# A two-layer graph network beside a mixing branch: all mixing moved into layer 0's gathers, the second layer finished tile by tile between the quads of its own gathers

## The reference

```
xn = layernorm(x)
# gnn, twice (W0, then W1), on xn:
  agg[r] = sum over edges (r, c) of v[c];  deg[r] = max(number of edges of r, 1)
  v = silu(layernorm((v + agg / deg) @ W.T + b) * g + beta)
# mix, on xn, row by row: logmap of xn, a 256 x 768 product with batchnorm folded in, relu,
  a grouped 128 x 128 product, an attention over groups of 32 channels,
  a 512 x 256 product, a tanh of the row's norm
x2 = x + gnn(xn) + mix(xn)
# ffn, on layernorm(x2): logits (6250 x 8 x 64), softmax, 8 x 64 slice tokens summed over ALL rows,
  a small attention between the tokens, and the result spread back over the rows
out = x2 + ffn
```

## Time and profile before

| | |
|---|---|
| median of 3 runs | 2936.33 us (2932.64 to 2941.06) |
| the profiled execution | 2949.13 us, of which the span from the first to the last instruction is 2947.2 us |
| first gather of layer 0 | 298.3 us |
| last product of layer 0 ends | 1308.0 us |
| first gather of layer 1 | 1432.0 us |
| last product of layer 1 ends | 2439.8 us |
| slice sums complete | 2799.6 us |
| mean granted TensorE clock | 0.873 of full speed |

### The profile page before, as it was taken

How to read it: one execution, slowest core, us unless ns; L and a number is a source line. 1 busy time by engine, 2 the same in 40 slices (tenths; PEclk the granted TensorE clock), 3 DMA queues, 4 the chain that set the end, 5 groups by cost and what they waited for, 6 DMA issues and landing times.

```text
span 2947.2 us, 34117 instructions
## 1 busy us (share of the span) xinstructions
PE 2224.6 (75%) x8923; PEld 1618.1 (55%) x8923; DVE 1404.6 (48%) x3188; ACT 1624.0 (55%) x3910; POOL 1645.6 (56%) x1745
## 2 busy tenths in 40 slices
PE   0776677777778787669487778778787658899999
PEld 0542456565656665555355656566565545455577
DVE  8899513443434443327523434344343215899611
ACT  7410465666666666536556666666666533565422
POOL 0000777777777777740477777777777771344300
PEclk9887688998888898878788989888898876899999
DMA  7200333333333333351333333333333347200002
GB/s 181 70 18 0 98 109 109 114 109 112 113 113 110 114 111 108 111 145 46 114 109 109 113 112 111 111 113 114 111 110 110 109 113 174 72 18 9 1 18 70
DMA packets 101271, 280.80 MB, mean 95 GB/s; under 512 B 29211, under 2 KB 43369, under 8 KB 97088
## 3 DMA queue, kind: packets, MB, share of 16 engines
q0 software_dynamic: 75904, 210.74, 25.1%
q1 hardware_dynamic: 12184, 55.08, 7.0%
q10 hardware_dynamic: 13000, 12.80, 1.5%
HBM read 252.91 MB, written 25.60 MB: 95 GB/s over the span
## 4 chain that ended last, share of the span: by engine, by line
POOL 50%; PE 17%; issue 17%; DVE 14%; DMA 1%; ACT 1%; DVEq 0%; ACTq 0%; SPq 0%; POOLq 0%
POOL big L566 50%; PE ps L1161 3%; PE ps L1262 3%; DVE arena_a L1296 3%; DVE arena_a L1297 3%; PE ps L1128 2%; PE ps L1150 2%; PE ps L1042 1%; PE ps L1144 1%; PE ps L1254 1%; PE ps L1159 1%; DVE big L1733 1%; DMA big<-table,arena_a 1%; DVE big L1734 1%; DVE lnst L1340 1%
## 5 line engine op out<-in xcount | busy, mean ns | idle before, releaser
L566 POOL DMA_INDIRECT big<-table,arena_a x1568 | 1509.6, 963 | 709.1 <-issue 476.7
L1042 PE MATMUL ps<-big 128*125 x3968 | 1073.5, 431 | 504.0 <-SPq L461 308.0
L1042 PEld LDWEIGHTS ps<-big 128*125 128x125 f32 x3968 | 833.3, 214 | 716.7 <-issue 565.4
L1629 DVE TENSOR_TENSOR big<-ps,big 125x257 f32 x496 | 211.0, 425 | 1263.5 <-PE ps L1042 1240.4
L697 ACT ACTIVATE arena_b<-iota_row,arena_a 128x125 f32<-128x125 f32 x1984 | 601.3, 386 | 62.2 <-PE ps L1042 28.2
L699 ACT ACTIVATE big<-arena_b,ones 128x1000 f32<-128x1000 f32 x248 | 280.0, 1129 | 8.1
L720 ACT ACTIVATE nodes<-nodes 125x512 f32<-125x512 f32 x50 | 31.6, 632 | 305.1 <-DVE nodes L1687 305.1
L1683 DVE RECIPROCAL nodes<-nodes 125x512 f32<-125x512 f32 x50 | 167.7, 3353 | 1.7
L1061 PE MATMUL ps<-arena_b,nodes 128*125 128x384 f32 x400 | 165.4, 538 | 0.0
L594 POOL TENSOR_TENSOR arena_b<-arena_b,head 125x512 f32<-125x512 f32 x50 | 55.0, 1100 | 161.9 <-DVE head L1741 161.9
L555 POOL IOTA big<- 1x992 f32 x1 | 0.9, 948 | 195.0 <-DVEq L1419 195.0
(11 more groups left out here) (387 smaller groups left out, 3159.7 us busy)
## 6 DMA issues: line engine op xcount, KB each, us to landing
big<-table,arena_a POOLq DMA_INDIRECT x1568
table<-nodes SPq DMA_DIRECT2D x9, 1120.0 KB
nodes<-table SPq DMA_DIRECT2D x4, 1680.0 KB
nodes<-table ACTq DMA_DIRECT2D x50, 125.0 KB
mix_rows<-nodes ACTq DMA_DIRECT2D x50, 125.0 KB
nodes<-in_x_dram SPq DMA_DIRECT2D x5, 1120.0 KB
big<-mix_rows SPq DMA_DIRECT2D x5, 1120.0 KB
nodes<-in_x_dram SPq DMA_DIRECT2D x10, 560.0 KB
```

What stands on the lines that cost most here:

```text
L566: pool.indirect_dma_start(gat[:, GRP * slot + k, 0:D], None, table[l], bass.IndirectOffsetOnAxis(ap=s_dst[:, n:n + 1], axis=0)).then_inc(s ...
L1042: mm = pe.matmul(ps[0:PT, SUM_BANKS[q % SB], 0:257], onehot[:, ROUND * (r % 2) + QS * k + n, :], gat[:, bass.ds(slots[QS * k + n], 1), :]. ...
L1629: dve.tensor_tensor(at, ps[0:PT, SUM_BANKS[q % SB], 0:257].unsqueeze(1), at, ALU.add).then_inc(s("agg_added"), 1)
```

## The change

Five things change together.

1. **Tiles are ranked by edge count.** After the layer norm's statistics VectorE makes the sizes of the tiles from the counts (ScalarE counts 33 bounds, VectorE 16 more), compares all 50 x 50 pairs, and for each tile makes a 125 x 800 bfloat16 mask times its rank, which TensorE adds up by 100 products with a unit matrix (`take_ranks`). The keys of the sort are built from these ranks, so levels 1 to 7 of the sort move behind all this and behind the row factors that followed the statistics. Small tiles come first. Idle quads are placed so that in layer 1 the tile of rank k is complete after 5 (k + 1) quads (`QUADS_A_TILE`).
2. **All 50 mixing tiles go into layer 0** (`NM = NT`). `window` now runs over 124 half rounds: two quads, then one slot, 111 slots in all. ScalarE makes its one-hot matrices two groups ahead. `mix_slot` keeps its steps, its order and its waits on all engines.
3. **Between the layers** the row factors of mixing and the weights of the logits are prepared, before TensorE's first quad of layer 1.
4. **Layer 1 goes tile by tile.** A list of 272 turns is worked out when the program is built (`second_layer_plan`). Each turn has one quad (as long as there are any, 248), and then steps of some tiles, in a fixed order: W slice sums, N division, M maximum, subtraction and exponential, L logits, D transpose for them, C scaled x2, Q and V second layer norm's roots, X x2, Z scale and tanh, R and S first layer norm's roots, B its statistics, H product with W1, T transpose, U agg / deg + x. Layer 1's quads have two banks (6, 7) in place of four; T, H and D share bank 5, L has bank 4 alone. GpSimd's division goes to VectorE. Each tile's rows of the layer-1 table, of x and of mixing are loaded by ScalarE's queue, and x2 is stored to DRAM by it. Part of the list (letter and rank):

The core of the diff:

```diff
-SUM_BANKS = (3, 4, 5, 7)
-SB = len(SUM_BANKS)
-IDLE_LOG = 12
-IDLE_STEP = 82
-assert 0 <= 50 * IDLE_STEP * NQ - NQ * 2 ** IDLE_LOG < 2 ** IDLE_LOG
+SUM_BANKS = ((3, 4, 5, 7), (6, 7))
+QUADS_A_TILE = 5
+SUMMED = 34
+EQ_RING = 4
 NSG = NSL // GRP
...
-NM = NT // 2
-EARLY = (0, 3)
+NM = NT
+HALVES = 2 * NSL // ROUND
+AHEAD = 2
...
+STAGES = ("W", "N", "M", "L", "D", "C", "Q", "V", "X", "Z", "R", "S", "B", "H", "T", "U")
+PE_COST = {"W": 1.9, "L": 1.0, "D": 0.35, "H": 1.4, "T": 0.35}
+DVE_COST = {"N": 1.6, "M": 1.5, "X": 1.8, "Z": 1.1, "S": 1.5, "V": 1.5, "B": 0.45, "U": 0.6}
+X1_RING, BASE_RING, XL_RING = 3, 3, 3
+
...
+                if st == "U" and tick < min(QUADS_A_TILE * (k + 1), NQ) - 1:
+                    break
+                if items and (pe + PE_COST.get(st, 0) > 2.3 or dve + DVE_COST.get(st, 0) > 3.1):
+                    break
+                if any(s0 == st for s0, _ in items) and st not in "SRVQ":
+                    break
+                pe, dve = pe + PE_COST.get(st, 0), dve + DVE_COST.get(st, 0)
+                at[st, k] = tick
+                items.append((st, k))
+                nxt[st] += 1
...
+def window(step, slot):
+
+
+    for half in range(max(HALVES, SLOTS)):
+        if half < HALVES:
+            step(half)
+        if half < SLOTS:
+            slot(half)
...
+                rows_dma(sp, x2_all[:, 10 * k:10 * k + 10, :], x2_d[:, 10 * k:10 * k + 10, :], s(f"nodes_back{k}"))
...
+            tile_of = tile_numbers(mybir.EngineType.SP)
+            for k in range(NT):
+                tile = tile_of(k)
+                sp.wait_ge(s("out_ready"), k + 1)
+                for p in PARTS:
+                    sp.dma_start(out_d[p, tile, :], x2_all[p, k, :].unsqueeze(1)).then_inc(s("out_stored"), 16)
...
+                def onehots_ahead(half):
+                    if half == 0:
+                        for grp in range(AHEAD):
+                            onehots(grp)
+                    if half + AHEAD < NSG:
+                        onehots(half + AHEAD)
...
+                def second_step(st, k):
+                    if st == "T":
+                        act.wait_ge(s("u_turned"), NT + k + 1)
+                        if k >= 2:
+                            act.wait_ge(s("h_made"), NT + k - 1)
+                        act.activation(uT_two[:, 2 * (k % 2):2 * (k % 2) + 2, :],
+                                       ps[:, 5, 0:D].rearrange("p (k c) -> p k c", k=2)[:, :, 0:PT], ACT.Copy).then_inc(s("bank5_read"), 1)
...
+                    if st == "C":
+                        act.wait_ge(s("xl_scaled"), GROUP_OF[k] + 1)
+                        if k >= XL_RING:
+                            act.wait_ge(s("w_used"), k - XL_RING + 1)
+                        act.activation(xl_ring[:, k % XL_RING, 0:D], acc[:, k, 0:D], ACT.Identity,
+                                       bias=xl_shift[:, k:k + 1], scale=cols[:, 2, k:k + 1]).then_inc(s("xl_ready"), 1)
...
+                    if st == "M":
+                        act.wait_ge(s("shifted"), k + 1)
+                        act.activation(ffw[:, k, :, :], ffw[:, k, :, :], ACT.Exp).then_inc(s("exp_done"), 1)
...
+                    if at >= len(banks):
+
+                        pe.wait_ge(s("agg_added"), q - len(banks) + 1)
...
+                    if st == "H":
+                        pe.wait_ge(s("bank5_read"), max(BANK_READS[st, k] - 1, BANK_READS["T", k]))
+                        pe.matmul(ps[0:PT, 5, 0:D], ones3[:, 0:PT], gbias3[1][:, :], start=True, stop=False)
+                        for n in range(2):
+                            mm = pe.matmul(ps[0:PT, 5, 0:D], uT_two[:, 2 * (k % 2) + n, :], wT[1][:, n, :], start=False, stop=(n == 1))
+                        mm.then_inc(s("h_made"), 1)
...
+                    if st == "L":
+                        pe.wait_ge(s("bank5_read"), BANK_READS["D", k])
+                        if k >= 1:
+                            pe.wait_ge(s("shifted"), k)
+                        pe.matmul(ps[0:PT, 4, :], ones3[:, 0:PT], lbias3[:, :], start=True, stop=False)
+                        for n in range(2):
+                            mm = pe.matmul(ps[0:PT, 4, :], xlT_ring[:, n, :], wc[:, n, :], start=False, stop=(n == 1))
+                        mm.then_inc(s("logits_made"), 1)
...
+            for t in range(SUMMED, NT):
+                link(dve.tensor_scalar(eq_ring[2 + t % 2], bin_b, float(t), 0.0, ALU.is_lt, ALU.add, accum_out=counts[0:PT, t:t + 1]))
...
+                link(dve.tensor_tensor(less, order.unsqueeze(1).to_broadcast([P, NT, NT]), order.unsqueeze(2).to_broadcast([P, NT, NT]), ALU.is_lt))
+                link(dve.tensor_reduce(rank, less, AX.X, ALU.add))
+                dve.sem_inc(s("ranks_ready"), 1)
+                for t in range(NT):
+                    if t >= EQ_RING:
+                        dve.wait_ge(s("eq_used"), t - EQ_RING + 1)
+                    dve.tensor_scalar(eq_ring[t % EQ_RING], bin_b, float(t), rank[0:PT, t:t + 1], ALU.is_equal, ALU.mult).then_inc(s("eq_made"), 1)
...
-                        dve.wait_ge(s("agg_made"), q + 1)
-                        dve.tensor_tensor(at, ps[0:PT, SUM_BANKS[q % SB], 0:257].unsqueeze(1), at, ALU.add).then_inc(s("agg_added"), 1)
...
+                    if st == "X":
+                        base = x_ring[:, k % BASE_RING, :]
+                        dve.wait_ge(s(f"base_row{k % BASE_RING}"), 32 * (k // BASE_RING + 1))
+                        do.mark(dve.scalar_tensor_tensor(out=base, in0=mix_ring[:, k % BASE_RING, :], scalar=by_rank[:, 0, k:k + 1], in1=base,
+                                                         op0=ALU.mult, op1=ALU.add))
+                        dve.wait_ge(s("tanh_done"), k + 1)
+                        do.mark(dve.scalar_tensor_tensor(out=row, in0=th_ring[:, k % 2, :], scalar=1.0, in1=row, op0=ALU.add, op1=ALU.mult))
+                        do.wait()
+                        dve.tensor_tensor(row, row, base, ALU.add).then_inc(s("x2_made"), 1)
+                        dve.wait_ge(s("x2_made"), k + 1)
...
+                    if st == "M":
+                        dve.wait_ge(s("logits_made"), k + 1)
+                        link(dve.tensor_reduce(head8[:, k % 2, 0, :], heads(ps[0:PT, 4, :]), AX.X, ALU.max))
+                        dve.wait_ge(s(f"x2_stored{k % 2}"), 16 * (k // 2 + 1))
+                        dve.tensor_tensor(each, logits, per_head(0).unsqueeze(3).to_broadcast([PT, 2, H // 2, G]), ALU.subtract).then_inc(s("shifted"), 1)
+                    if st == "N":
+                        dve.wait_ge(s("exp_done"), k + 1)
+                        link(dve.tensor_reduce(per_head(1), each, AX.X, ALU.add))
+                        link(dve.reciprocal(head8[:, k % 2, 2, :], head8[:, k % 2, 1, :]))
...
+                    for tick, items in enumerate(PLAN):
+                        if tick < NQ:
+                            addition(tick)
+                        for st, k in items:
+                            second_step(st, k, tick)
```

More of the change, by code:

```diff
@@ L170, in group_due, with roots_due, h_bank @@
     return g if rest == 0 and 0 <= g < NT // 10 else None
[L173 to L183, removed]
+def roots_due(i):
+    return 1 + min(max((i - (LN_Z - 2)) // 10 + 1, 0), NT // 10)
+def h_bank(a):
+    return 3 if a % 2 == 0 else 7
 def live(i, lag, n=NT):
@@ L414, in run_halves, with tile_numbers, tile_of @@
             return g[:, :, 0:gap], g[:, :, gap:2 * gap]
+        def tile_numbers(engine):
+            held = {}
+            def tile_of(k):
+                part = k // 16
+                if part not in held:
+                    held.clear()
+                    _, held[part] = nc.values_load_multi_w_load_instructions(
+                        order_row[0:1, part * 16:min(part * 16 + 16, NT)], [engine], min_val=0, max_val=NT - 1,
+                        skip_runtime_bounds_check_because="a tile's number, a sum of one-hot products")
+                return bass.ds(held[part][k % 16], 1)
+            return tile_of
         block = ctx.enter_context(nc.Block())
@@ new lines, in _ @@
+            sp.wait_ge(s("ffn_loaded"), 8 * 16)
+            tell_landed(1, 0)
+            for first in range(0, NGRP - RG, 16):
+                quads_before = free_slots(1, first)
+                for grp in range(first, min(first + 16, NGRP - RG)):
+                    tell_landed(1, grp + 1)
+                    sp.wait_ge(s("agg_made"), quads_before[grp - first])
+                    sp.sem_inc(s("slots_free"), 1)
+            for grp in range(NGRP - RG + 1, NGRP):
+                tell_landed(1, grp)
@@ L819, in post_slot @@
+                        act.activation(nodes[:, b, :], acc[:, b, 0:D], ACT.Silu).then_inc(s("silu_done"), 1)
                     a = tile_at(i, 1)
                     if a is not None:
[L821 to L827 removed]
@@ new lines, in _ @@
+                if l == 0:
+                    window(products, mix_slot)
+                    pe.wait_ge(s("gw_ready"), 4)
```

(11 more changed lines are left out.)

956 lines of the change are left out of this document (533 added, 423 removed).

## The result

The changed kernel takes 3030.78 us (median of 4 runs, 3012.33 to 3031.4) where the kernel before takes 2938.69 beside it: a ratio of 1.030, interval 1.026 to 1.034. I forecast 2885 with a range up to 2985 and gave a slower kernel 0.26. The sign is wrong and the time lies outside the range.

What follows compares the result with a forecast made beforehand. GpSimd's gathers were taken to bound both gather stages. The terms 50 + 155 + 30 - 283 - 3 gave -51 us, so 2885 us against the median of 2936.3, with a range of 2795 to 2985.

Steps and rivals of the forecast that it cites:

- Preparation, +50: Before the first gather: counts, tile ranking and masks make the stage 50 us longer, bounds +38 and +65.
- Layer 0's gathers, +155: Layer 0's gather stage, now with all 50 mixing tiles, grows by 155 us, bounds +105 and +270.
- a tenth more on 9.1: 19.7 us: Layer 0's period per mixing tile: TensorE's 9.1 us cost a tenth more for its clock, making 19.7 us.
- the circle: Layer 0's loop of waits through ScalarE, TensorE and VectorE: 18.7 us per tile at full clock, above the supply of 16.0.
- Layer 1's gathers, +30: Layer 1's gather stage, with mixing gone and the old end moved in, grows by 30 us, bounds 0 and +120.
- turns slower than gathers: Rival, chance 0.24: layer 1's turns take 4.5 us in the mean, not 4.0, costing 120 instead of 30: 2975 us.
- 30 turns take 113 against 120: Layer 1, from turn 111: thirty turns need 113 us against 120 of gather supply, so gathers still set the pace.
- turns 111 to 121: Layer 1's turns, some with N, M and L in series at 8.0 us: together about 49 us against 44 of supply.
- Between the layers, 0: From layer 0's gathers to layer 1's: new VectorE work of some 35 us is covered by the ring, costing 0.
- after the last quad, -283: Layer 1's end: 24 remaining turns take 77 us in place of 359.8, bounds -311 and -259.
- Tail, -3: The kernel's last stage: same products, stores hidden, the last one smaller, so 3 us less, bounds -5 and +25.
- Late ScalarE: Rival, chance 0.07: in layer 1, 48 table loads at twice 1.28 us each delay ScalarE: about 2940 us.

Runs made afterwards that it cites:

- Experiment 3: Changed kernel with unread spare products filling TensorE's stalls in both layers, all orders kept: 2917.5 us, ratio 0.993 to the kernel before.
- experiment 2: Changed kernel with only VectorE's order in layer 1 changed, M ahead of the quad's addition and N: 2922.4 us, ratio 0.994 to the kernel before.
- the first try: Changed kernel with thirteen spare products in layer 0 only, behind the wait for `rT_ready`, on the chip with gaps: 3507 us, ratio 1.078.
- The same kernel: Changed kernel with only VectorE's order in layer 0 changed, odd slot before its additions: 3339 us on the chip with gaps, 2820.5 us elsewhere, ratio 0.959.

## Why the prediction was wrong

**Preparation, +50, came as +43.** Right in its steps: level 8 of the sort began at 127.8 (134 forecast). The masks were the term that I had too high, 25 us for 50; one kept VectorE busy for 0.42, and the next began 0.34 after it:

```profile
L1524 DVE TENSOR_SCALAR arena_b<-arena_b 125x800 bf16<-125x800 bf16 x26 | 10.1, 424 | 0.6 <-PE ps L1041 0.2 <-DVE arena_b L1532 0.2 <-DVE arena_b L1519 0.2
```

The whole run of masks, from 59.1 to 77.7, is 18.6 us long. The Trainium skill's estimate by "VectorE: DVE Perf Modes" (14 us, the part +40) was nearer to these 18.6 us than my value from 32-bit rows.

**Layer 0's gathers, +155, came as +213.** The mechanism was right, link for link, and GpSimd's waits for `slots_free` came as told. The term that failed is the clock's in the period, "a tenth more on 9.1: 19.7 us": I gave it 1.0 us, and it is 1.6, with 0.2 more in the other links. A full period is 20.6 to 20.7 us. I had spread the granted clock of 0.89 evenly, from a mean over 500 us. The loss is not even: it sits right behind the stall of the circle, which means wholly inside the circle. Experiment 3 shows that with its 75.6 us. The 49 periods from the first `o_ready` (431.5) to the last (1433.7) take 1002 us for my 965, the last two of them only 15 and 14 each: 37 of the 58 us. The other 21 lie ahead of the first `o_ready` (13) and behind the last (8), and I did not follow them.

The Trainium skill ("TensorE: Matmul & The Clock Gate", section "HAM oscillation — how this bites in real kernels") describes this pattern, products in groups with waits between them that bring the engine back to its lower clock. This case's trace agrees, with 0.55 behind a wait of 3.5 us. I had not asked which link stands behind the wait.

**Layer 1's gathers, +30, came as +108.** The rival "turns slower than gathers" is what happened, nearly to the number: 1115.6 / 248 = 4.50 us a turn, and 120 us was its price. The step that failed is "30 turns take 113 against 120", and in it the first part, turns 111 to 121 "to about 49". They took 63.6. Some 6 of the 15 are my own sum: at the prices I gave (two turns of 8.0, two of 6.6, seven of 3.7) they are 55. Of the other 9, some 3 are the clock (1.5 us in each of the two turns with N, M and L), 2 the two turns with M and L (6.9 and 8.2 us), and 4 turn 115, which took 7.4 for my 3.7: TensorE stood still for 2.0 us ahead of the next quad, and the quad took 3.25 us at a granted clock of 0.59, where the quad at 2193.38 took 1.89.

```profile
2206.40 3.25 PE L1219 MATMUL ps<-whole 128*125 x8 [2.02 <-issue]
```

The nine turns after them took 26.4 for my 27; the turns with X and Z and those after them 49 for 37. So 139 us for 120 of supply. The margin of 7 us was less than the error of the sum. The end of the list I had too dear: from the addition of turn 228 to that of turn 247 are 87 us, for the 100 that I gave to 228 to 247.

A second fault lies in the reasoning. I let light turns make up for heavy ones. They can't win back what GpSimd lost: when it doesn't wait, its gathers start 1.25 us apart (median), in this kernel as in the one before, so what it lost by standing still, 113 us in all, stays lost, and the stage grew by 108. Only the ring's depth covers a burst.

**Between the layers, 0, and after the last quad, -283**, came as -1 and -283, the second with 24 turns in 76.7 us for my 77. That close a hit is luck: I had picked the 77 between a chain of 63 at full clock and a line of 101, and worked out neither the clock nor the waits there.

**Tail, -3, came as +2.** The hundred stores were hidden: SyncE issued the two of a tile within 0.8 us, under the 2.2 us of a tile. Where the other 5 us went was not followed.

**Late ScalarE** didn't happen. Layer 1 has 34 table loads of 1.28 us. In 23 of them the activation starts 0.01 us behind the load's end (1987.23 behind 1985.94 and 1.28), in the other 11 it waits for VectorE, and with them in place experiment 2 reached the pace of the gathers.

**What the forecast lacked altogether** is the remedy that lay beside the circle. I listed that `additions` stand ahead of VectorE's odd slot, and took it as given.

## What to carry to other kernels

Add up the links around each loop of engines that wait for each other, not only each engine's work, and then ask of each link whether it must wait for the one before or only stands behind it in the program. Price the link behind a stall of TensorE at its lower clock, since a mean clock spreads that loss over work that isn't in the loop. Where a supplier with a short buffer sets the pace, compare it with demand burst by burst, because light stretches give back nothing that the supplier lost by standing still.

## What the runs showed of the hardware

- A stall of 3.5 us left TensorE at a granted clock of 0.55 for the next 3.1 us, a stall of 3.75 us at 0.56. Filling both kinds of stall with useless products made a kernel of 3031 us one of 2917.5.
- Equal stalls need not cost the same. Behind waits of 2.8 to 2.95 us the thirteen spare products of the first try took 4.5 to 4.8 us in 18 cases and 3.14 in 11 (granted clock 0.64 and 1.00 where it was read), and 3.06 with no wait ahead of them.
- The same kernel took 3339 us on one chip and 2820.5 on another, the kernel before 3228.7 and 2938. On the slower one TensorE stands still in the middle of a quad, between single products, with nothing in the profile to wait for. Why stays open; nothing in these traces tells.
